# Turning the pair products two columns at a time: S as stationary operand of 128 columns, U with two sides of 192 rows

## The reference

```python
e = jnp.stack([tbl_0[ids[:, 0]], ..., tbl_25[ids[:, 25]]], axis=1)          # 2048 x 26 x 128
combined = jnp.concatenate([dense_output[:, None, :], embeddings], axis=1)   # 2048 x 27 x 128
interactions = jnp.einsum('bfd,bgd->bfg', combined, combined)
iu, ju = jnp.triu_indices(27, k=1)                                           # 351 pairs
z = jnp.concatenate([dense_output, interactions[:, iu, ju]], axis=1)
h = jnp.concatenate([z, r_dense_output], axis=1)                             # 607 columns
h = jnp.maximum(h @ W_top1 + b_top1, 0.0)                                    # 512
h = jnp.maximum(h @ W_top2 + b_top2, 0.0)                                    # 256
y = h @ W_top3                                                               # 2048 x 1
```

## Time and profile before

| what | value |
|---|---|
| time, median of 3 runs | 523.08 us (521.77 to 524.66) |
| profiled execution, its own time | 513.81 us |
| span of its trace | 512.0 us |
| TensorE matmul busy | 408.9 us, 80% |
| VectorE busy | 245.8 us, 48% |
| GpSimd busy | 263.1 us, 51% |
| ScalarE busy | 136.1 us, 27% |
| mean granted TensorE clock | 0.917 |

### The profile page before, as it was taken

The page is one execution under the profiler, slowest core; times in us unless marked ns, Lnnn a source line. Parts: engine busy times, 40 slices in busy tenths (PEclk is TensorE's granted clock), DMA queues, the critical chain, the costliest instruction groups (busy, mean ns, idle before and its releaser), DMA issues.

```text
span 512.0 us, 10047 instructions
## 1 busy us (share of the span) xinstructions
PE 408.9 (80%) x4352; PEld 362.6 (71%) x4352; DVE 245.8 (48%) x312; ACT 136.1 (27%) x356; POOL 263.1 (51%) x280
## 2 busy tenths in 40 slices
PE   2885387857979688879878799797887968887998
PEld 2664366746867578768867678686776857886976
DVE  5994127554445454446453454545543454433332
ACT  2451112321223222223212322233212222123531
POOL 6787464552556636454635646264463654635000
PEclk9997596978999799998989979898998979989999
DMA  7978112221212212221212212123121221211000
GB/s 197 249 187 258 36 47 67 70 67 42 63 42 86 84 33 65 61 87 49 68 43 72 73 53 68 37 83 83 49 57 52 70 65 49 57 32 53 3 12 1
DMA packets 20133, 36.74 MB, mean 72 GB/s; under 512 B 6157, under 2 KB 9877, under 8 KB 20090
## 3 DMA queue, kind: packets, MB, share of 16 engines
q0 software_dynamic: 8704, 17.84, 12.7%
q1 hardware_dynamic: 5338, 9.08, 6.8%
q10 hardware_dynamic: 6048, 9.18, 5.9%
HBM read 36.07 MB, written 0.01 MB: 70 GB/s over the span
## 4 chain that ended last, share of the span: by engine, by line
PE 61%; another core or an unknown queue 13%; issue 12%; DVE 10%; ACT 2%; DMA 1%; SPq 0%; ACTq 0%; DVEq 0%
PE psB L382 23%; PE psG L408 14%; DVE one_hot L646 7%; PE psB L453 7%; PE psB L366 5%; PE psB L460 4%; PE psB L418 2%; PE psB L447 2%; DVE tab_lo L651 2%; PE psB L432 2%; DMA ET<-tbl 1%; PE psB L465 1%; DVE ZH L510 1%; ACT ET L553 1%
## 5 line engine op out<-in xcount | busy, mean ns | idle before, releaser
L307 POOL DMA_INDIRECT E<-tbl,gidx x272 | 262.3, 964 | 206.7 <-PE psB L366 109.7
L646 DVE TENSOR_TENSOR one_hot<-oidx,psR 125x1024 fp32r<-125x1024 int32 (+1 forms) x152 | 179.2, 1189 | 116.3 <-remote 60.4
L382 PE MATMUL psB<-one_hot,tab_hi 125*128 125x256 f32 x592 | 117.9, 321 | 19.0 <-ACT tab_hi L535 9.4
L408 PE MATMUL psG<-ET 128*52 128x52 f32 x2048 | 81.9, 228 | 44.4 <-issue 35.7
L382 PE MATMUL psB<-one_hot,tab_lo 125*128 125x256 f32 x592 | 105.4, 302 | 5.6 <-issue 4.7
L408 PEld LDWEIGHTS psG<-ET 128*52 128x52 f32 x2048 | 67.8, 139 | 59.2 <-issue 54.5
L382 PEld LDWEIGHTS psB<-one_hot,tab_hi 125*128 125x128 f32 x592 | 88.4, 206 | 27.3 <-issue 20.5
L382 PEld LDWEIGHTS psB<-one_hot,tab_lo 125*128 125x128 f32 x592 | 90.1, 208 | 9.1 <-issue 7.5
L669 DVE COPY_PREDICATED S<-second,psG 116x208 f32<-116x208 int32 x64 | 25.0, 391 | 103.1 <-ACT S L582 94.0
L582 ACT COPY S<-psG 116x208 f32<-116x208 f32 x64 | 21.2, 333 | 146.6 <-remote 82.0
L553 ACT COPY ET<-psB 128x512 f32<-128x512 f32 (+3 forms) x80 | 44.3, 572 | 50.9 <-PE psB L366 30.9
(11 more groups left out here) (46 smaller groups left out, 188.7 us busy)
## 6 DMA issues: line engine op xcount, KB each, us to landing
oidx<-hot_idx ACTq DMA_DIRECT2D x28, 256.0 KB
E<-tbl,gidx POOLq DMA_INDIRECT x272
ET<-tbl SPq DMA_DIRECT2D x3, 448.0 KB
oidx<-hot_idx SPq DMA_DIRECT2D x4, 256.0 KB
dense<-dense_pairs SPq DMA_DIRECT2D x8, 128.0 KB
ZH<-tbl SPq DMA_DIRECT2D x2, 448.0 KB
S<-tbl SPq DMA_DIRECT2D x2, 448.0 KB
oidx<-hot_idx ACTq DMA_DIRECT2D x7, 128.0 KB
```

Of the source, the lines that this page charges most:

```text
L307: nc.gpsimd.indirect_dma_start(E[:, n % SLOTS, i, :], None, gathered[feature_and_tile(n, i)[0]], bass.IndirectOffsetOnAxis(ap=gidx[:, 4 * ...
L382: product = nc.tensor.matmul(bank[:, t % 2 * DUO:(t % 2 + 1) * DUO], tab[0:ROWS_P, TABLE_BASE[t] + k0 + i, :], one_hot[0:ROWS_P, m % RING, ...
L408: gram = nc.tensor.matmul(psG[g % 2][q * LANE:q * LANE + M, a * M:(a + 1) * M], two[:, 0:M], two[:, PAIR:], start=True, stop=True)
L646: nc.vector.tensor_tensor(one_hot[0:ROWS_P, m % RING, 0:many], ids, rows, ALU.is_equal).then_inc(hot_full[m % RING], 1)
```

## The change

S is laid out with the two duos outermost, so that two columns of one duo lie side by side: 2 x 64 = 128 stationary columns. A C step now turns up to 4 "twos" of columns, and there are 13 transposes in 4 C steps (4, 4, 4 and 1) where there were 26 in 7. The result has 128 partitions: the first column of each two on partitions 0 to 63, the second on 64 to 127. U becomes 128 partitions by 4 x 192 rows. ScalarE empties C steps 0 and 2, VectorE 1 and 3; the copies (8 for a duo, as before) are of 8, 16, 64, 96, 128, 160, 192 and 104 elements where they were 16 to 384. The split steps become two: step 0 turns the first 128 rows of both sides with 4 transposes of 128 by 128, into 512 columns; step 1 turns the last 64 rows of each side, the lower side with 4 transposes of 64 by 64 and the upper side, which has to come out on partitions 64 to 127, with 4 matmuls against the identity. The two kinds alternate. ScalarE's and VectorE's splitting works on 512 and then 256 columns. The host lays the first weight matrix out to suit.

```diff
-    COLUMNS = [range(c, min(c + 4, F)) for c in range(1, F, 4)]
-    BLOCKS = [range(1, 3), range(3, 5)] + COLUMNS[1:]
+    TWOS = (F - 1) // 2
+    COLUMNS = [range(t, min(t + 4, TWOS)) for t in range(0, TWOS, 4)]
+    BLOCKS = [range(0, 1), range(1, 2)] + [range(t, min(t + 2, TWOS)) for t in range(2, TWOS, 2)]
...
     def splits(d):
-        return [("split", d, kp) for kp in range(KP)]
+        return [("split", d, i) for i in range(2)]
...
-        S = sb("S", [P, F - 1, 2, DUO_J], f32)
+        S = sb("S", [P, 2, F - 1, DUO_J], f32)
...
-                for i, c in enumerate(COLUMNS[b]):
-                    turned = nc.tensor.transpose(bank[0:DUO_J, i * P:i * P + MT], S[0:MT, c - 1, d % 2, :],
-                                                 ident[0:MT, 0:MT])
+                for i, t in enumerate(COLUMNS[b]):
+                    two = S[0:MT, d % 2, 2 * t:2 * t + 2, :].rearrange("p f j -> p (f j)")
+                    turned = nc.tensor.transpose(bank[:, i * P:i * P + MT], two, ident[0:MT, 0:MT])
...
                 for v in range(GROUP):
-                    turned = nc.tensor.transpose(bank[:, v * DUO_J:(v + 1) * DUO_J],
-                                                 U[0:DUO_J, v, kp * P:(kp + 1) * P], ident[0:DUO_J, 0:DUO_J])
+                    if i == 0:
+                        turned = nc.tensor.transpose(bank[:, v * P:(v + 1) * P], U[:, v, 0:P], ident[:, :])
+                        continue
+                    low, high, samples = slice(0, DUO_J), slice(DUO_J, P), slice(v * DUO_J, (v + 1) * DUO_J)
+                    nc.tensor.transpose(bank[low, samples], U[low, v, P:PAIRS // 2], ident[low, low])
+
+                    turned = nc.tensor.matmul(bank[high, samples], U[high, v, P:PAIRS // 2], ident[high, high],
+                                              start=True, stop=True)
...
-                            wait_out(pe, ("split", d, kp))
+                            wait_out(pe, ("split", d, kp // 2))
...
-                n, high, base = len(block), block[-1], block_base[block]
+                n, high, base = len(block), 2 + 2 * block[-1], block_base[block]
                 at = block[0] - COLUMNS[b][0]
-                turned = bank[0:DUO_J, at * P:(at + n) * P].rearrange(
-                    "p (c h f s) -> p h s f c", c=n, h=2, s=PAIR)[:, :, :, 0:high]
-                rows = U[0:DUO_J, :, base:base + n * high].rearrange("p (h s) (f c) -> p h s f c", h=2, c=n)
+                turned = bank[:, at * P:(at + n) * P].rearrange(
+                    "p (t h f s) -> p h s t f", t=n, h=2, s=PAIR)[:, :, :, :, 0:high]
+                rows = U[:, :, base:base + n * high].rearrange("p (h s) (t f) -> p h s t f", h=2, t=n)
...
-                nc.scalar.copy(Zp_hi[:, kp, :], pairs_as_rows(d, kp)).then_inc(Zp_hi_ready, 1)
+                nc.scalar.copy(rows_of(Zp_hi, i), pairs_as_rows(d, i)).then_inc(Zp_hi_ready, 1)
...
-                split = nc.vector.tensor_tensor(Zp_lo[:, kp, :], pairs_as_rows(d, kp),
-                                                Zp_hi[:, kp, :].bitcast(f32), ALU.subtract)
+                split = nc.vector.tensor_tensor(rows_of(Zp_lo, i), pairs_as_rows(d, i),
+                                                rows_of(Zp_hi, i).bitcast(f32), ALU.subtract)
```

More of the change, by code:

```diff
@@ L76, in dlrm_program @@
         block_base[block] = rows_so_far
-        rows_so_far += len(block) * block[-1]
-    assert rows_so_far == PAIRS
+        rows_so_far += len(block) * (2 + 2 * block[-1])
+    assert 2 * rows_so_far == PAIRS
     def columns(d):
@@ L429, in turn_pairs @@
                         pe.wait_ge(bank_out[bank], count)
-                bank, full = wait_empty(pe, ("split", d, kp))
+                bank, full = wait_empty(pe, ("split", d, i))
                 for v in range(GROUP):
-                    turned = nc.tensor.transpose(bank[:, v * DUO_J:(v + 1) * DUO_J],
-                                                 U[0:DUO_J, v, kp * P:(kp + 1) * P], ident[0:DUO_J, 0:DUO_J])
+                    if i == 0:
+                        turned = nc.tensor.transpose(bank[:, v * P:(v + 1) * P], U[:, v, 0:P], ident[:, :])
[4 more added lines that the diff above has]
+                                              start=True, stop=True)
                 turned.then_inc(full, 1)
@@ L504, in empty_columns, with pairs_as_rows, rows_of @@
                     continue
-                n, high, base = len(block), block[-1], block_base[block]
+                n, high, base = len(block), 2 + 2 * block[-1], block_base[block]
                 at = block[0] - COLUMNS[b][0]
-                turned = bank[0:DUO_J, at * P:(at + n) * P].rearrange(
-                    "p (c h f s) -> p h s f c", c=n, h=2, s=PAIR)[:, :, :, 0:high]
-                rows = U[0:DUO_J, :, base:base + n * high].rearrange("p (h s) (f c) -> p h s f c", h=2, c=n)
+                turned = bank[:, at * P:(at + n) * P].rearrange(
+                    "p (t h f s) -> p h s t f", t=n, h=2, s=PAIR)[:, :, :, :, 0:high]
+                rows = U[:, :, base:base + n * high].rearrange("p (h s) (t f) -> p h s t f", h=2, t=n)
                 copied = nc.scalar.copy(rows, turned) if eng is nc.scalar else nc.vector.tensor_copy(rows, turned)
             copied.then_inc(emptied, 1)
-        def pairs_as_rows(d, kp):
-            return psB[PLACE["split", d, kp][0]][:, 0:DUO]
+        def pairs_as_rows(d, i):
+            bank = psB[PLACE["split", d, i][0]]
+            if i == 0:
+                return bank[:, :].rearrange("p (v k j) -> p k v j", v=GROUP, k=2)
+            return bank[:, 0:DUO].rearrange("p (k v j) -> p k v j", k=1, v=GROUP)
+        def rows_of(split, i):
+            return split[:, 0:2 if i == 0 else KP].rearrange("p k (v j) -> p k v j", v=GROUP)[:, 2 * i:]
         def empty_part(eng, d, p):
@@ L582, in empty_gram_first, with round_pairs @@
                 nc.scalar.copy(gram_rows(d, i), gram_samples(g, 0)).then_inc(G_first[g % 2], 1)
-            def round_pairs(d, kp):
-                wait_full(act, ("split", d, kp))
-                if kp == 0 and d:
+            def round_pairs(d, i):
+                wait_full(act, ("split", d, i))
+                if i == 0 and d:
                     wait_full(act, ("part", d - 1, M1 - 1))
-                if kp == 0:
+                if i == 0:
                     act.wait_ge(Zd_in, 16 * (d + 1))
                     nc.scalar.copy(Zd_hi[:, :], Zd[:, :]).then_inc(Zd_hi_ready, 1)
-                nc.scalar.copy(Zp_hi[:, kp, :], pairs_as_rows(d, kp)).then_inc(Zp_hi_ready, 1)
+                nc.scalar.copy(rows_of(Zp_hi, i), pairs_as_rows(d, i)).then_inc(Zp_hi_ready, 1)
             def load_Zd(d):
@@ L745 @@
     W1 = x["W_top1"]
-    blocks = [(1, 3), (3, 5)] + [(c, min(c + 4, F)) for c in range(5, F, 4)]
-    rows = []
+    twos = (F - 1) // 2
+    blocks = [(0, 1), (1, 2)] + [(t, min(t + 2, twos)) for t in range(2, twos, 2)]
+    rows = [[], []]
     for low, high in blocks:
-        for f in range(high - 1):
-            for c in range(low, high):
-                a, b = sorted((order[f], order[c]))
-                rows.append(W1[128 + int(first[a]) + b - a - 1] if f < c else _np.zeros_like(W1[0]))
+        for t in range(low, high):
+            for f in range(2 * high):
+                for side in range(2):
+                    c = 1 + 2 * t + side
+                    a, b = sorted((order[f], order[c]))
+                    rows[side].append(W1[128 + int(first[a]) + b - a - 1] if f < c else _np.zeros_like(W1[0]))
+    rows = rows[0][:128] + rows[1][:128] + rows[0][128:] + rows[1][128:]
     arrays = {
```

17 lines of the change are left out of this document (8 added, 9 removed).

## The result

| | before | after |
|---|---|---|
| time, median of 4 runs each | 522.42 us (521.62 to 524.66) | 534.53 us (529.96 to 537.81) |
| ratio | | 1.0351 [1.0245, 1.0457] |
| profiled execution, own time | 513.81 us | 536.42 us |
| span, mean granted clock | 512.0 us, 0.917 | 534.6 us, 0.875 |
| end of the last matmul | 510.10 us | 532.68 us |

Slower by 12.1 us, where 5 us faster was forecast. From the traces I take where time goes, from the medians how much.

A forecast was written before the change was run, and what follows sets the result against it. TensorE, the busiest engine, was taken to bound the kernel, with its waits and low clock. 0.8 - 5.4 - 0.4 = -5.0 us took the profiled 513.81 to 508.8; adding the median's 9.3 gave 518 us, range 509 to 528.

The forecast's parts named there:

- C steps: TensorE's C transposes, 26 becoming 13, still 0.099 us apart: 1.29 us saved for a duo.
- Split steps: TensorE's split steps, 0.80 us before, 2.20 after with 0.12 us for each of 8 changes: +1.40 us for a duo.
- TensorE's own sum: C and split steps together +0.11 us for a duo, +0.8 in seven duos; the tail counted apart, -0.37 us.
- Waits, -5.4 us: TensorE's waits in duos' turnings: three series become single waits, 1.8 us saved each; bounds 0 and -16 us.
- My term for the clock: Behind three merged waits, clock 0.76 instead of 0.52 over 7 us: 1.7 us of full clock each, half counted.
- T steps and parts, 0: T steps and second-layer parts move a place or two among hot chunks: 0, a badly placed T step at most 3 us.
- Rival 2: Slower: each change between low and high costs 0.175 us and waits don't shrink: 527 us, chance 0.20.
- Rival 1: Changing between low and high in the split steps costs nothing: -12 us, 511 us, chance 0.24.
- Rival 3: Late signals keep their pace, the wait at split step 0 absorbs TensorE's changes, only the tail remains: 522.7 us, chance 0.18.

The follow-up runs named there:

- e5_after: The changed kernel run again unchanged, signals prompt: 386.09 us, 1.0056 of before.
- e6_before: The kernel before run again unchanged, signals prompt: 387.41 us, from two runs only.
- d2: The changed kernel with seven idle copies put ahead of ScalarE's last C copy in six duos, signals prompt: 427.05 us, 1.1059 of before.
- d4: The changed kernel with both sides of split step 1 as matmuls and seven idle ScalarE copies added in six duos, prompt: 407.24 us, 1.0625 of before.
- e1b: The changed kernel with planner weights restoring the order of before but for a few hot steps, signals late: 559.31 us, 1.0623 of before.
- e9: The changed kernel with split step 1 all matmuls and planner weights restoring the order of before, signals late: 535.82 us, 1.0118 of before.
- e7b: The changed kernel with both sides of split step 1 as matmuls, still alternating, signals late: 534.91 us, 1.022 of before.
- e8_before_order: The kernel before with planner weights giving T steps, parts and hot steps the changed kernel's order, signals late: 1.039 of before.
- e2: The changed kernel with split step 1 grouped, four low transposes and then four high matmuls, signals prompt: 380.54 us, 0.9888 of before.
- e7: The changed kernel with both sides of split step 1 as matmuls, still alternating, signals prompt: 380.56 us, 0.9906 of before.
- e1_weights: The changed kernel with planner weights putting T steps and parts among hot steps as before, signals prompt: 389.87 us, 1.0145 of before.

## Why the prediction was wrong

- **C steps: right.** 13 transposes 0.10 us apart: nine take (1.06 - 0.26) / 8 = 0.10. The Trainium skill (TensorE: Matmul & The Clock Gate, LDWEIGHTS) gives 107 ns for a load of 128 columns. No such pace shows: the trace after has these transposes 100 ns apart, and the earlier trace rows others with 128 columns 67 apart.
- **Split steps: right at full clock.** Forecast 2.20 us with 0.12 for a change, measured 2.25 to 2.27 and 0.13. At half clock they take 3.6, and that is where six of eight now run.
- **TensorE's own sum, +0.11 us a duo and -0.37 in the tail: right in sign, too small.** Prompt, where little else counts, it gives +0.4 us; measured is +0.56%, about 2 us. The period of the middle five duos is 44.26 us (e5_after) against 43.88 (e6_before), both at full clock, so +0.38 a duo. Counted from each record's start to the next one's, the C steps are 1.25 us shorter (forecast 1.29) and the split steps 1.38 longer (1.40). What is missing are the T steps, 0.30 us longer: 0.08 because these five duos hold one T step more, the rest because of where they stand. Such a step takes 0.36 us with a hot step behind it and 0.53 with a gram behind it, and ten of them have a gram behind them where seven had.
- **Waits, -5.4 us: this step failed.** "I give a single wait no gain, and a series one the difference." The form was forecast, one wait of about 3 us ahead of split step 0. The six pieces came out at 2.3 to 6.4 us, mean 4.3, and TensorE's idle time in a duo's turning at 4.0 to 5.2 us where it had been 3.5 to 4.2 (second to sixth duo), so no wait was saved. A gain had been read off the seventh duo's 2.91 us, during which the last gather of all was issued; the third and fifth duo, in which the prediction also saw no series, idle 4.1 and 3.5 us in their turning, about as much as the series' 3.6 to 4.2. Above all the clock behind the wait was taken from a row of before, 0.76 behind the earlier trace rows's single wait, as though what runs behind it were unchanged. Behind it now stand sixteen short records with changes between them, the clock is low for 10.2 us, and over the whole trace for 133 us instead of 85. My term for the clock has the wrong sign. That the step behind the wait alone moves the clock is shown by d2 against d4 (the same wait) and by e1b against e9 (nearly the same); in the change's own order late, e7b doesn't show it beyond its scatter.
- **T steps and parts, 0: this failed too**, shown by e8_before_order (+3.9%), which changes the order alone. How much of the 12 us is this step and how much the one above stays open.
- **Rival 2** (slower, 527 us) was right in sign and in "the series may reappear as one long wait at split step 0"; its price, 0.175 for a change and no loss by the wait, was not the mechanism. **Rival 1** is refuted in its time by e2: in the step as it was written a change costs 0.13 us. Its reason, that the two halves alternate freely, holds for matmuls (e7). **Rival 3** said that the signals come at their own pace, which the rows below bear out; but the time did not stay the same.
- The range ended at 528 because no case let the wait grow or the low clock last longer. That term was bounded by 16 us of gain on one side and by 0 on the other: a loss was left out, although rival 2 spoke of a wait that returns.

## What to carry to other kernels

A wait of TensorE is paid twice, once as idle time and once as low clock behind it, and the second part depends on what stands behind the wait: with one and the same 21.5 us of waits, 54.6 us of low clock behind them with the alternating step and 20.5 with matmuls alone. Make neighbouring small operations one kind (a transpose can be written as a matmul against the identity): 0.13 us for each change of kind, and here 5.5 us of the prompt kernel. When several short waits are merged into one, price the merged one with its own clock, and bound it on both sides of zero. And when a change alters the counts that a planner spreads its steps by, try the new order with the old instructions: here that alone cost 3.9% late.

## What the runs showed of the hardware

**Late signals.** VectorE and ScalarE in the third duo of the trace after, and then GpSimd:

```profile
237.21 1.22 DVE L663 TENSOR_TENSOR one_hot<-oidx,psR 125x1024 fp32r<-125x1024 int32 x1 [2.33 <-remote]
240.03 0.46 DVE L519 COPY ZH<-psB 128x96 f32<-128x96 f32 x2 [1.59 <-remote]
241.50 0.27 DVE L519 COPY ZH<-psB 128x104 f32<-128x104 f32 x1 [1.02 <-remote]
```

```profile
241.47 0.29 ACT L519 COPY ZH<-psB 128x160 f32<-128x160 f32 x1 [6.43 <-remote]
```

```profile
237.60 0.95 POOL L310 DMA_INDIRECT E<-tbl,gidx  x1 [0.30 <-issue]
238.85 0.94 POOL L310 DMA_INDIRECT E<-tbl,gidx  x1 [0.30 <-issue]
252.42 0.94 POOL L310 DMA_INDIRECT E<-tbl,gidx  x1 [12.62 <-PE psB L369]
```

TensorE's last C transpose ends at 236.09. ScalarE, idle for 6.43 us, begins its copy at 241.47, 2.6 us after GpSimd began its last gather of a row; the earlier trace rows's copy came 4 us late, and the last gather of before began 2.6 us ahead of it, at 469.73. Matched one by one with the ends of the transposes, the semaphore updates of C steps (those on record; the late traces lack some) come 3.0 us (median) and up to 6.1 us late in this trace, and at most 0.02 late in e5_after, though GpSimd issues gathers there at the same 1.25 us from one to the next. For transposes behind the last gather (493.19) no update is late. So lateness goes with the gathers, and with something that differs between sessions, which no run here shows; none takes the gathers away. I put the difference between 384 and 523 us for one kernel down to it, as the program is the same, but no run hastens or delays the signals alone.

**GpSimd waits for it too.** Its idle time ahead of gathers is 84 us, nearly all with nobody named, in e5_after, and 232 in the trace after, of which 135 are put down to TensorE's transposes. The last gather above waited 12.62 us for them. It looks as if late signals of T steps held the gathers back. The two rows of the pages, e5_after and after:

```profile
L310 POOL DMA_INDIRECT E<-tbl,gidx x272 | 263.3, 968 | 84.4 <-issue 82.3
```

```profile
L310 POOL DMA_INDIRECT E<-tbl,gidx x272 | 260.8, 959 | 231.7 <-PE psB L369 135.1
```

**A transpose and a matmul of 64 by 64 don't mix, two matmuls do.** It is 0.13 us for each change of kind (e1_weights against e2_grouped), against 0.06 us from one pair of matmuls to the next in the two halves of the array (e7_both_matmul).
